# A recommendation tower on one core: field dots in column tiles, six fields looked up by matmul, a ring of 13 gathered rows

## The reference: what is computed

```python
e = jnp.stack([tbl_0[ids[:, 0]], ..., tbl_31[ids[:, 31]]], axis=1)   # 2048 x 32 x 256
dots = jnp.einsum('bnd,bmd->bnm', e, e)[:, iu, ju]                    # the 496 pairs i < j
h = jnp.concatenate([dots, dense_ctx], axis=1)                        # 2048 x 512
h = jnp.maximum(h @ W_top1 + b_top1, 0.0)                             # 512 -> 512
h = jnp.maximum(h @ W_top2 + b_top2, 0.0)                             # 512 -> 256
y = h @ W_top3                                                        # 256 -> 1
```

## Time and profile before

| | |
|---|---|
| median of three runs | 623.67 us |
| the profiled execution: its own time, its span | 627.5 us, 625.7 us |
| TensorE clock granted, mean share of full speed | 0.988 |
| PE busy | 563.3 us, 90% of the span |
| POOL busy | 436.8 us, 70% |
| DVE busy, ACT busy | 365.1 us (58%), 285.1 us (46%) |
| DMA | 69.79 MB, mean 112 GB/s |

### The profile page before, as it was taken

One profiled execution on the slowest core, in us unless ns is written; L12 is line 12 of the kernel. 1 busy time (PEld: TensorE's weight loads), 2 busy tenths in 40 slices (PEclk: granted clock), 3 DMA queues, 4 the chain that ended last, 5 costly groups with the idle time before them and its releaser, 6 DMA issues.

```text
span 625.7 us, 11900 instructions
## 1 busy us (share of the span) xinstructions
PE 563.3 (90%) x4864; PEld 555.9 (89%) x4864; DVE 365.1 (58%) x802; ACT 285.1 (46%) x503; POOL 436.8 (70%) x454
## 2 busy tenths in 40 slices
PE   0269999999999999999999999999999899998973
PEld 0259999989999999999999999999999899998973
DVE  3165847657483856658483857658483575835330
ACT  0173545544363544545364544545354354545330
POOL 6788777777777777777777777777777777775000
PEclk9999999999999999999999999999999899999997
DMA  7982343455344644455343643455343743354000
GB/s 174 230 272 74 113 116 113 115 78 151 107 115 114 114 116 113 116 80 149 107 119 111 115 114 115 115 79 148 110 119 108 112 118 105 110 88 107 2 1 0
DMA packets 35600, 69.79 MB, mean 112 GB/s; under 512 B 15590, under 2 KB 20198, under 8 KB 35046
## 3 DMA queue, kind: packets, MB, share of 16 engines
q0 software_dynamic: 21504, 58.75, 37.7%
q1 hardware_dynamic: 14042, 10.28, 6.9%
HBM read 68.98 MB, written 0.01 MB: 110 GB/s over the span
## 4 chain that ended last, share of the span: by engine, by line
POOL 45%; PE 29%; issue 15%; DMA 5%; DVE 4%; ACT 1%; DVEq 0%
POOL rows L234 45%; PE gram_ps L270 12%; PE sel_ps L324 6%; PE tr_ps L249 5%; DMA rows<-in_tbl,ids_sb 4%; PE gram_ps L292 4%; PE gram_ps L302 2%; DVE sel_low L424 1%; DVE onehot L437 1%; PE gram_ps L281 0%; DVE emb_t L366 0%; DVE dots L383 0%; ACT dots L383 0%; DVE dots_t L445 0%; PE gram_ps L310 0%
## 5 line engine op out<-in xcount | busy, mean ns | idle before, releaser
L234 POOL DMA_INDIRECT rows<-in_tbl,ids_sb x448 | 436.1, 973 | 137.5 <-issue 135.0
L270 PE MATMUL gram_ps<-emb_t 128*128 128x124 f32 x2048 | 240.2, 276 | 0.3 <-DVE y_sb L472 0.3
L270 PEld LDWEIGHTS gram_ps<-emb_t 128*128 128x128 f32 x2048 | 235.2, 193 | 0.6 <-issue 0.4
L366 DVE COPY emb_t<-tr_ps 128x512 f32<-128x512 f32 x112 | 127.8, 1141 | 67.7 <-PE tr_ps L249 66.8
L383 ACT COPY dots<-gram_ps 32x124 f32<-32x124 f32 x256 | 96.0, 375 | 132.6 <-PE gram_ps L270 130.4
L249 PE MATMUL tr_ps<-ident,rows 128*128 128x128 f32 x896 | 120.8, 280 | 37.3 <-DMA rows<-in_tbl,ids_sb 37.3
L366 ACT COPY emb_t<-tr_ps 128x512 f32<-128x512 f32 x112 | 128.2, 1145 | 54.1 <-PE tr_ps L249 52.7
L249 PEld LDWEIGHTS tr_ps<-ident,rows 128*128 128x128 f32 x896 | 104.6, 146 | 39.6 <-DMA rows<-in_tbl,ids_sb 20.1
L324 PE MATMUL sel_ps<-onehot,sel_high 125*128 125x256 f32 x512 | 126.4, 287 | 7.2 <-DVE emb_t L373 6.3
L383 DVE COPY dots<-gram_ps 32x124 f32<-32x124 f32 x256 | 94.6, 370 | 55.3 <-PE gram_ps L270 52.7
L324 PE MATMUL sel_ps<-onehot,sel_low 125*128 125x256 f32 x512 | 124.0, 283 | 0.0
(11 more groups left out here) (19 smaller groups left out, 108.2 us busy)
## 6 DMA issues: line engine op xcount, KB each, us to landing
rows<-in_tbl,ids_sb POOLq DMA_INDIRECT x448, 2.8
sel_ids<-in_ids_by_field SPq DMA_DIRECT2D x32, 128.0 KB, 3.5
emb_t<-in_tbl SPq DMA_DIRECT2D x4, 896.0 KB
w_sb<-in_W_top SPq DMA_DIRECT2D x1, 1024.0 KB
w_sb<-in_W_top SPq DMA_DIRECT2D x1, 512.0 KB
emb_t<-in_tbl SPq DMA_DIRECT2D x4, 104.0 KB
packed<-in_dense_ctx SPq DMA_DIRECT2D x16, 8.0 KB
ids_sb<-in_ids SPq DMA_DIRECT2D x1, 240.0 KB, 3.0
```

Source lines behind the costliest of these rows:

```text
L234: pool.indirect_dma_start(out=rows[g % RING][:, j, :], out_offset=None, in_=tables[f], in_offset=bass.IndirectOffsetOnAxis(ap=ids_sb[:, t, ...
L270: last = nc.tensor.matmul(gram_out[k][:, g, :], four.rearrange("p s f -> p (s f)"), four[:, :, 0:firsts], start=(h == 0), stop=(h == D_HAL ...
L366: copy(emb_t[t % PAIR][:, h, :, at[0]:at[-1] + 1].rearrange("p (g s) f -> p f s g", s=QUAD), tr_ps[h][g % 2][:].rearrange("p f (s g) -> p ...
```

## The change

- **Column tiles.** A gram matmul takes two samples in place of four: 64 stationary columns and 62 moving ones, and the two pairs of samples of a group write to partitions 0 to 63 and 64 to 127 of the bank. There are twice as many matmuls with half the columns on either side. A bank now holds 8 groups, so there are 4 fills a tile, and the copies out are half as many and twice as long (32 x 8 x 31).
- **Six selected fields.** 19 and 20 join the four. 26 fields are gathered: six quads of four and one of two. The select jobs become 48, six a pair of tiles: two in the odd period, four in the even one. There is one `onehot` buffer instead of two, in two halves that are handed back one by one (`half_selected`).
- **A ring of 13 rows** instead of 8 quads (32 rows); POOL waits row by row for the quad that last used the slot.
- **The order.** PE, DVE and ACT get a new hand-written order for a pair of periods, 6 quads in the odd and 8 in the even one, and the transposes run 4 quads ahead: 11 quads are transposed before period 1. The first pair's select jobs lie between these.
- **The start.** SP loads each table after the first only when the gathered quad before it has landed. The tables have a place of their own rather than `emb_t[1]`.
- **The end.** Layer 3 is turned round: one stationary column, 128 moving ones, one row of 128 results, which is written out for every tile by one DMA of 512 bytes. The dense numbers are loaded once for all tiles, and `packed`, `feat_t` and `hid1_t` share memory with `dots` and `dots_t`.

The core of the diff:

```diff
-SELECTED = (22, 24, 27, 31)
+SELECTED = (19, 20, 22, 24, 27, 31)
 SELECT_CHUNKS = 8
-RING = 8
+RING = 13
 SPRAY = 16
+TILED = 2
+EARLY = 2
+AHEAD = 4
...
-    bank_groups = 4
+    bank_groups = 8
...
 
-        p, at = (t + 1) // PAIR, range(0, early) if t % PAIR else range(early, n_sel)
+
+        p, at = (t + 1) // PAIR, range(0, EARLY) if t % PAIR else range(EARLY, n_sel)
...
+    turns_at_start = quads + AHEAD
+    turns_odd, turns_even = 6, 8
+
+    def quad_turned(t, at):
+
+        pairs_before, odd = divmod(t - 1, PAIR)
+        g = turns_at_start + pairs_before * (turns_odd + turns_even) + odd * turns_odd + at
+        return g if g < len(every_quad) else None
+
...
-        rows = [sbuf(f"rows{r}", [P, QUAD, width]) for r in range(RING)]
+        rows = sbuf("rows", [P, RING, width])
...
-        onehot = [sbuf(f"onehot{s}", [select_rows, SELECT_CHUNKS, pair_cols], f32r) for s in range(2)]
+        onehot = sbuf("onehot", [select_rows, SELECT_CHUNKS, pair_cols], f32r)
...
+            load_table(0)
+            for n in range(1, n_sel):
+                sp.wait_ge(rows_loaded[(n - 1) % quad_sems], rows_landed(n - 1) * DMA)
+                load_table(n)
...
+                sp.wait_ge(y_copied, t)
+                sp.dma_start(y[(t - 1) * P:t * P, :].rearrange("s o -> o s"), y_sb).then_inc(y_stored, DMA)
...
-                wait(pool, transposed[1], g - RING + 1)
-                for j, place in enumerate(places(k)):
+                for slot, place in zip(slots(g), places(k)):
+                    j = t * n_rows + place - RING
+                    if j >= 0 and quad_of_row(j) >= freed:
+                        freed = quad_of_row(j) + 1
+                        pool.wait_ge(transposed[1], freed)
...
-                        four = emb_t[u][:, h, s:s + QUAD, :]
-                        last = nc.tensor.matmul(gram_out[k][:, g, :], four.rearrange("p s f -> p (s f)"),
-                                                four[:, :, 0:firsts], start=(h == 0), stop=(h == D_HALVES - 1))
+                        for c in range(0, QUAD, TILED):
+                            own = emb_t[u][:, h, s + c:s + c + TILED, :]
+                            last = nc.tensor.matmul(gram_out[k][c * fields:(c + TILED) * fields, g, :],
+                                                    own.rearrange("p s f -> p (s f)"), own[:, :, 0:firsts],
+                                                    start=(h == 0), stop=(h == D_HALVES - 1))
...
-                    last = nc.tensor.matmul(mlp_ps[0][:, 0:1], hid2_t[:, i, :], w3_sb[:, i:i + 1],
+                    last = nc.tensor.matmul(mlp_ps[0][0:1, 0:P], w3_sb[:, i:i + 1], hid2_t[:, i, :],
...
+                    if h == 0:
+                        pe.wait_ge(onehot_built[half], j + 1)
+                    for c in range(half * part, (half + 1) * part):
                         for table in (sel_high, sel_low):
                             last = nc.tensor.matmul(sel_ps[j % 2][:, h, :], table[:, i, c, h * P:(h + 1) * P],
-                                                    onehot[j % 2][:, c, :], start=(c == 0 and table is sel_high),
+                                                    onehot[:, c, :], start=(c == 0 and table is sel_high),
                                                     stop=(c == SELECT_CHUNKS - 1 and table is sel_low))
-                last.then_inc(selected, 1)
...
+                    if h == 1:
+                        last.then_inc(half_selected[half], 1)
...
+            def odd_period(t):
...
+                gram(t - 1, 0)
+                select(early[0], 0)
+                turning(0)
+                gram(t - 1, 1)
+                select(early[0], 1)
+                turning(1)
+                gram(t - 1, 2)
+                gram(t - 1, 3)
+                turning(2)
+                for h in range(D_HALVES):
+                    select(early[1], h)
                 turn(t - 1)
-                turning(5)
+                turning(3)
                 if t == 1:
                     pe.wait_ge(weights_loaded, 5 * DMA)
                 layer1(t - 1)
+                turning(4)
+                layer2(t - 1)
+                transpose(quad_turned(t, 5), 0)
+                layer3(t - 1)
+                transpose(quad_turned(t, 5), 1)
+
...
+            def even_period(t):
...
+                gram(t - 1, 0)
+                gram(t - 1, 1)
+                turning(0)
+                gram(t - 1, 2)
+                gram(t - 1, 3)
+                turning(1)
+                for h in range(D_HALVES):
+                    select(late[0], h)
+                turn(t - 1)
+                turning(2)
+                layer1(t - 1)
+                turning(3)
+                layer2(t - 1)
+                select(late[1], 0)
+                layer3(t - 1)
+                select(late[1], 1)
+                turning(4)
+                for h in range(D_HALVES):
+                    select(late[2], h)
+                turning(5)
+                select(late[3], 0)
                 turning(6)
-                layer2(t - 1)
+                select(late[3], 1)
                 turning(7)
...
+            first_jobs = jobs(0)
+            for g in range(turns_at_start):
+                for h in range(D_HALVES):
+                    transpose(g, h)
+                for job in first_jobs[g - 2:g - 1] if g >= 2 else []:
+                    for h in range(D_HALVES):
+                        select(job, h)
...
+                wait(dve, half_selected[half], j)
+                for c in range(part):
```

More of the change, by code:

```diff
@@ L209, in _ @@
                 sp.dma_start(b2_sb[:], b2.rearrange("(k p) -> p k", p=P)).then_inc(weights_loaded, DMA)
-            load_ctx(0)
+            for job in jobs(0)[4:]:
+                load_sel_ids(*job)
             for job in jobs(1):
@@ L326, in select @@
                                                     stop=(c == SELECT_CHUNKS - 1 and table is sel_low))
-                last.then_inc(selected, 1)
-            def period(t):
-                turning = (lambda k: transpose(t, k)) if t < tiles else (lambda k: None)
-                now = jobs(t)
-                for k in range(fills_each):
-                    turning(k)
-                    gram(t - 1, 2 * k)
-                    gram(t - 1, 2 * k + 1)
-                turning(4)
-                for job in now[:1]:
-                    select(*job)
+                    if h == 1:
+                        last.then_inc(half_selected[half], 1)
@@ L345, in period @@
                 turning(6)
-                layer2(t - 1)
+                select(late[3], 1)
                 turning(7)
-                for job in now[1:]:
-                    select(*job)
-                layer3(t - 1)
             pe.wait_ge(ident_ready, 1)
-            for k in range(quads):
-                transpose(0, k)
-            for job in jobs(0):
-                select(*job)
-            for t in range(1, tiles + 1):
-                period(t)
-        def emb_copy(eng, h, copy, t, k):
-            if t >= tiles or k >= quads:
+            first_jobs = jobs(0)
@@ L363, in emb_copy @@
+            for g in range(turns_at_start):
+                for h in range(D_HALVES):
+                    transpose(g, h)
+                for job in first_jobs[g - 2:g - 1] if g >= 2 else []:
+                    for h in range(D_HALVES):
+                        select(job, h)
+            for t in range(1, tiles + 1, PAIR):
+                odd_period(t)
+                even_period(t + 1)
+        def emb_copy(eng, h, copy, g):
+            if g is None:
                 return
-            g, at = t * quads + k, places(k)
+            (t, k) = every_quad[g]
+            at = places(k)
@@ L426, in split_table, with build_onehot @@
                                         ).then_inc(tables_split, 1)
-            def build_onehot(p, i, half):
-                j = job_number(p, i)
+            def build_onehot(job, half):
+                if job is None:
+                    return
+                j = job_number(*job)
                 if half == 0:
@@ L444, in spread @@
                     dve.wait_ge(dots_copied[k], (t + 1) * fills_each)
[L445 to L462 removed]
+                nc.vector.transpose(dots_t[:, 0:firsts * fields], dots_sb[:]).then_inc(dots_spread, 1)
@@ new lines, in _ @@
+            first_jobs = jobs(0)
+            for half in range(2):
+                build_onehot(first_jobs[0], half)
+            next_jobs = first_jobs[1:] + jobs(1)[:1]
+            for g in range(turns_at_start):
+                emb_copy(dve, 0, copy, g)
+                if 1 <= g <= n_sel:
+                    split_table(g - 1)
+                for job in next_jobs[g - 2:g - 1] if g >= 2 else []:
+                    for half in range(2):
+                        build_onehot(job, half)
@@ L490, in _ @@
+            dve.wait_ge(weights_loaded, 5 * DMA)
+            dve.wait_ge(ctx_loaded, DMA)
+            for t in range(1, tiles + 1, PAIR):
```

(26 more changed lines are left out.)

314 lines of the change are left out of this document (185 added, 129 removed).

## The result

The kernel with the change took 604.73 us (median, 604.58 to 607.08) against 624.58 us of the kernel before in the same comparison: a ratio of 0.968 (0.964 to 0.973), 3.2% faster. The forecast was 585 us. The direction holds and 604.7 us lies inside the range, but only half of the gain that was forecast came.

The account below looks back on a forecast made before the run. PE (71.1 us a pair) and POOL (70.0) were taken as nearly tied. 75 us to period 1, seven pairs of 66, 24 for period 15 and 26 after gave a 587 us span, median 585; range 567 to 635.

Parts of the forecast that it names:

- PE's and POOL's work in a pair: Per pair of tiles: PE falls from 71.1 to 66 us, POOL from 70.0 to 65.0, again tied.
- The single `onehot` buffer: DVE's builds for the selects: waiting for PE's use counted as nothing; 6.8 us a pair if every build were exposed.
- Column tiles: Gram records on PE: 27.9 ns if two tiles work at once, 55.8 in turns, 111.6 without a fall; 27.9 taken.
- The change of tiling mode: Entering and leaving the tiled grams on PE: ten drains of 0.17 us, 1.7 us a pair, perhaps nothing.
- The ring: POOL's 13 rows ahead: PE may be 8.5 us late, largest lag some 4 us, so no cost.
- The start: Until period 1: 75 us, between 71.5 and 79, 14 later than before, with 12 to 20 us lost by POOL.
- Period 15 and the end: Last stretches of the span: period 15 takes 24 us instead of 29.1, what follows 26 instead of 37.8.
- Serial tiles: Rival in the gram stretches: tiles take turns at 55.8 ns a record, pair 80.3 us, median 698; chance 0.15.
- partly concurrent ones: Rival in the gram stretches: tiles partly at once, 38 to 42 ns a record, 612 to 635 us; chance 0.08.
- The starving ring: Rival at the short ring: late quads stop POOL 4 to 5 us a pair, 607 to 618 us; chance 0.12.
- the likeliest case: Whole kernel: the forecast together with the variant where POOL alone sets the pace, 573 to 606 us; chance 0.62.

Follow-up runs that it names:

- e9: The kernel of e5 with the three small loads (W_top3, two biases) issued right behind the first table instead of behind the weights: 584.36 us, 0.9335.
- the order experiment: The changed kernel with each fill's gram matmuls reordered, all of the lower column tile first, then all of the upper: 700.7 us, ratio 1.116.
- e1: The changed kernel with the ids of select jobs 2, 3 and 4 loaded between the tables instead of behind the weights: 590.5 us, ratio 0.940.
- e5: The kernel of e1 with 16 thrown-away identity products on PE in each of the last two periods: 587.39 us, 0.938.
- e7: The kernel of e1 with the tables' low parts made by a plain copy instead of a subtraction: 592.53 us, 0.946.
- after: The kernel with the whole change as first made, against the kernel before: 604.73 us, ratio 0.968.

## Why the prediction was right, and where it was wrong

**PE's and POOL's work in a pair: right.** A near tie at 66 and 65 was forecast; PE's 66.2 was measured, and with four fields POOL's 70.05. The single `onehot` buffer, which the sum put at nothing, cost nothing: between 182 and 513 us PE never waits for it. Adding up the distances between PE's starts over one pair of the changed kernel gives 15.7 us for the grams (forecast 14.3), 24.4 for the selects (23.5), 13.4 for the transposes with their waits (11.3), 7.2, 3.6 and 2.0 for the layers and the turn.

**Column tiles: right, by the lowest of three prices.** 30.6 ns a record against 27.9, and 55.7 when the tiles take turns, against 55.8. By the distances between starts, the rule of the Trainium skill ("TensorE: Matmul & The Clock Gate", Part 3: Packing small matmuls) that a load overlaps only across row groups does not hold here: tiles that share all rows and differ in columns do overlap.

The reason given for the price was only half right. The prediction read from layer 3's single moving column that the price "hangs mainly on the 128 stationary columns being loaded, not on what is moved". The kernel's own new layer 3 has it the other way round, one stationary column and 128 moving ones, and its records start 108 ns apart (row 313.30 above and nine more places). The old layer 3's start 112 ns apart once the first is through; its 92 ns are a mean that the first record lowers. So either side alone at 128 columns keeps the price near 110 ns. The tiled gram got cheap because both sides were halved, 128 to 64 and 124 to 62; no run halves one side alone.

The change of tiling mode, which drains the engine by the Trainium skill ("TensorEngine Tiling (Array Packing)", Key Properties), was priced at 1.7 us a pair, and the trace agrees with something of that size. From the start of the last transpose to the first gram record lie 203 ns, where it was 109 before (25 places between 182 and 513 us). From the start of the last gram record to the next transpose or select lie 152 ns, where the records of a fill lie 29 apart. That is 0.22 us for entering and leaving, 1.1 us a pair for five of each. Layer 3 with its one column shows about 0.09 us on each side as well, 0.4 us a pair, which the sum didn't have.

**The ring: right.** The leave was enough, at no cost: POOL stops for about 1.2 us a pair (66.2 against its own 65.0) because it is the faster engine, and PE never waits for rows.

**The start: wrong, and this is the step that failed.** "I take 75" was the term, with 71.5 to 79 as its bounds (its own parts add up to 70.9 to 78.9); it measured 85.7, past the 80 us that the prediction had named as a sign of being wrong. I counted what POOL needs to issue 42 gathers and let DVE's table work hold it for 12 to 20 us. I didn't follow SP's queue. The prediction says of the tables' staggered load that it "costs nothing in this sum: its cover is that POOL's 54 us are longer than the transfers take". That looked at the tables alone. The last of them was issued only at 39.7 us, when its quad had landed, and everything behind it in SP's queue waited too. In the new order these are 1.5 MB of weights and behind them the ids of the third and later jobs (before, the ids stood ahead of the weights; the list of the changes above leaves this out), and the start's selects, which now lie between the transposes, need them one by one. With three of these loads moved, period 1 began at 75.3 us. That this is the forecast's 75 is luck: the sixth job's ids still came late, and POOL's own loss was less than the 12 to 20 us of the term. With the small loads first (e9) POOL lost 9.4 us until its 42nd gather, and period 1 began at 69.5, below the term's lower bound.

**Period 15 and the end: near.** 26.1 and 25.5 us were measured against 24 and 26. The store fell to 1.4 us, below the 2.5 taken. In period 15 the slow layer 1 came a second time (5.55 us): before, transposes lay between the tile's last gram and layer 1, and 3.57 us was its price there. I kept the slow price for the last period and not for this one.

**The rivals.** Serial tiles and partly concurrent ones are excluded by the 30.6 ns and the order experiment. The starving ring is seen with 9 rows, not with 13. That 604.7 us lies inside the likeliest case, 573 to 606, is luck: its upper end was not drawn for a queue wait of 10 us, which no case had.

## What to carry to other kernels

A small f32 matmul gets cheaper when both its stationary and its moving columns shrink; here one side alone at 128 columns kept it at 108 to 112 ns a record. It gets cheaper again if its neighbour in program order lies in another column tile; check that by reordering alone. Engine time freed on one of two tied engines is worth next to nothing until work is moved from the other (0.7% here). When start-up work is interleaved with a pipeline, follow every small load through its queue: a load that one engine needs next, behind megabytes that nobody needs yet, stops all of them in turn through a short ring.

## What the runs showed that I had not expected

- Gram matmuls of 32 by 31 in four tiles cost 12.3 ns a record where they ran without holes, and PE then stopped for up to 2.8 us with nothing in the profile to wait for.
- Whichever load SP issued behind the last table, the weights and the dense numbers was held for 10 to 12 us while the DMA engines were full: W_top3 in e1, e5 and e7, the ids of a select job in after and e9. W_top3 issued at the very start took 1.1 us (e9).
- One stationary column and 128 moving ones cost 108 ns a record, as much as 128 stationary columns and one moving one.
- Selects at the start ran at 213 ns a record where the granted clock was at the lower level, 1.2 GHz (e1, 53.9 to 57.3 and 65.3 to 71.0 us), against about 120 ns in the middle of the span at 2.4 GHz. From 57 to 64 us, just before the clock fell for the second time, PE was busy for 2.8 us of 7.
- The same program began period 1 up to 7.6 us apart in two executions.
